# A GRU kernel in which TensorE gets the new state as two summands, and a search whose sums are queued inside the next products

## The reference, cut to what matters

```python
# block 1: a weighted outer product, of which the 5120 largest of each batch's 512 x 512 values become 1, the rest 0
adj = fside * cond[:, None, :] * softmax(x, -1) / sqrt(512);  adj[diagonal] = -inf
x = x + top_k_mask(adj, 5120)
# block 2: attention with 16 heads, conditioned norm
x = x + attention_block(x, cond, ...)
# block 3: a GRU over the 512 rows of x, starting from cond
for t in range(512):
    gi = x[:, t] @ W_ih + b_ih;  gh = h @ W_hh + b_hh
    r = sigmoid(i_r + h_r);  z = sigmoid(i_z + h_z);  n = tanh(i_n + r * h_n)
    h = (1 - z) * n + z * h;  hs[:, t] = h
x = x + hs
# block 4: linear sampling of x along its columns at places given by cond
```

## Time and profile before

| | |
|---|---|
| three runs | 2466.45, 2470.41, 2475.15 us (median 2470.41) |
| profiled execution | 2475.3 us, of which the span of instructions 2473.6 |
| PE busy | 2243.5 us, 91% of the span, 58517 matmuls |
| DVE busy | 1854.6 us, 75% |
| ACT busy | 1295.0 us, 52% |
| POOL busy | 532.7 us, 22% |
| granted TensorE clock, mean | 0.991 |

### The profile page before, as it was taken

One profiled execution on the slowest core, in us unless ns is written; L12 is line 12 of the kernel. 1 busy time (PEld: TensorE's weight loads), 2 busy tenths in 40 slices (PEclk: granted clock), 3 DMA queues, 4 the chain that ended last, 5 costly groups with the idle time before them and its releaser, 6 DMA issues.

```text
span 2473.6 us, 139634 instructions
## 1 busy us (share of the span) xinstructions
PE 2243.5 (91%) x58517; PEld 1912.7 (77%) x58517; DVE 1854.6 (75%) x8525; ACT 1295.0 (52%) x5693; POOL 532.7 (22%) x2223
## 2 busy tenths in 40 slices
PE   2668899898987899999999999999999999999998
PEld 2564454555544598988999999999999999999996
DVE  7876877868679588877787777777777768777775
ACT  5564856848557444444445454444444445444443
POOL 1001011020113323333222222222222222222221
PEclk9999899999999999999999999999999999999999
DMA  5000000010010000000000000000000000000000
GB/s 189 3 2 1 1 1 1 2 52 1 1 52 1 18 5 5 5 5 5 5 5 5 9 9 5 9 9 5 9 5 9 9 5 9 9 5 9 5 13 20
DMA packets 8444, 32.08 MB, mean 13 GB/s; under 512 B 836, under 2 KB 904, under 8 KB 7560
## 3 DMA queue, kind: packets, MB, share of 16 engines
q1 hardware_dynamic: 7392, 23.07, 2.5%
q10 hardware_dynamic: 424, 0.07, 0.0%
HBM read 18.94 MB, written 4.19 MB: 9 GB/s over the span
## 4 chain that ended last, share of the span: by engine, by line
PE 48%; DVE 9%; issue 2%; ACT 1%; POOL 1%; DVEq 0%; POOLq 0%
PE psum L1790 41%; PE psum L1723 5%; PE psum L1750 2%; DVE keepB L1423 1%; ACT mixA L822 1%; DVE nlineA L1415 1%; DVE nlineB L1415 1%; DVE rzA L1400 1%; PE psum L1472 1%; DVE keepA L1423 1%; POOL region_rows L486 1%; DVE parts1A L1432 0%; DVE parts0A L1432 0%; DVE lineA L1439 0%; DVEq L1431 0%
## 5 line engine op out<-in xcount | busy, mean ns | idle before, releaser
L1790 PE MATMUL psum<-parts0A,region_w_hh 128*128 128x40 f16 x12288 | 432.5, 179 | 16.2 <-DVE parts0A L1448 10.1
L1790 PE MATMUL psum<-parts1A,region_w_hh 128*128 128x40 f16 x12288 | 433.2, 179 | 15.3 <-DVE parts1A L1448 10.8
L1790 PE MATMUL psum<-parts1B,region_w_hh 128*128 128x40 f16 x12288 | 433.2, 179 | 7.3 <-issue 1.7
L1790 PE MATMUL psum<-parts0B,region_w_hh 128*128 128x40 f16 x12288 | 432.7, 179 | 7.4 <-DVE parts0B L1448 2.5
L822 ACT ACTIVATE mixA<-rzA 128x8 f32<-128x8 f32 x512 | 110.8, 216 | 564.3 <-DVE rzA L1400 564.1
L1790 PEld LDWEIGHTS psum<-parts0A,region_w_hh 128*128 128x128 f16 x12288 | 372.7, 96 | 25.6 <-DVE parts0A L1448 15.8
L1790 PEld LDWEIGHTS psum<-parts1A,region_w_hh 128*128 128x128 f16 x12288 | 373.3, 96 | 24.7 <-DVE parts1A L1448 16.7
L1790 PEld LDWEIGHTS psum<-parts0B,region_w_hh 128*128 128x128 f16 x12288 | 362.7, 96 | 26.2 <-DVE parts0B L1448 6.4
L1790 PEld LDWEIGHTS psum<-parts1B,region_w_hh 128*128 128x128 f16 x12288 | 362.7, 96 | 25.6 <-DVE parts1B L1448 6.0
L1400 DVE TENSOR_REDUCE rzA<-psum 128x8 f32<-128x32 f32 x512 | 97.6, 191 | 185.9 <-PE psum L1790 176.3
L497 POOL TENSOR_TENSOR addA<-zA,lineA 128x8 f32<-128x8 f32 x512 | 104.4, 204 | 586.8 <-ACT zA L829 586.8
(11 more groups left out here) (259 smaller groups left out, 4006.2 us busy)
## 6 DMA issues: line engine op xcount, KB each, us to landing
region_rows<-in_x_dram SPq DMA_DIRECT2D x4, 1024.0 KB, 12.4
out_dram<-region_w_b SPq DMA_DIRECT2D x16, 256.0 KB, 2.0
region_w_a<-in_L_cond_W_qkv_dram SPq DMA_DIRECT2D x1, 3072.0 KB, 22.7
region_w_hh<-in_L_cond_W_hh_dram SPq DMA_DIRECT2D x4, 768.0 KB, 7.2
region_rows<-in_L_cond_W_ih_dram SPq DMA_DIRECT2D x1, 3072.0 KB, 10.1
region_cond<-in_cond_dram SPq DMA_DIRECT2D x2, 1024.0 KB, 6.4
region_cols<-in_L_cond_W_emb_dram SPq DMA_DIRECT2D x1, 2048.0 KB, 18.4
region_w_out<-in_L_cond_W_out_dram SPq DMA_DIRECT2D x1, 1024.0 KB, 21.5
```

The source lines that it names most:

```text
L1790: made = e.matmul(k.slots(bank)[:, :, ch, :, 0:2], k.w16[:, 2 * read + c, part, NC * "rzn".index(g) + 2 * half + ch], k.parts[now][read][: ...
```

## The change

PE now multiplies the state as a sum of two terms that were never added for it: z h, and keep times tanh. Each has a high and a low fp16 part, so a chunk has 16 columns instead of 8, and with `COPIES` = 2 a matmul has 32 columns instead of 40. A group in PSUM is six columns: four products, the constant, the input's share; sums and the n line run over 48 columns.

POOL makes z h in fp32 (`zh`), the same product in fp16 (`zhigh`), and their difference (`zlow`), straight into the parts that PE reads; its copies to the array of states are gone. DVE makes keep times tanh in fp16 (`dve_high`) and in fp32 (`dve_cand`), both plain products of 8 columns, their difference (`dve_low`), and the state as `cand + zh` (`dve_state`), off the way to PE: that of A behind keep B, that of B behind low B. High no longer waits for z h. PE waits for `low` and `zlow` of a half. The products run through PSUM, so the state is still the sum.

In the search, PE does the first 10 of the 16 pieces of count n, then the total of count n - 1, then the other 6. The totals lie in banks 4 to 7 now, and `pe_embed`, which uses bank 7, waits until the last sign is made.

```diff
--- before.py
+++ after.py
@@ -40,7 +40,8 @@
 FAR = 2.0 ** 24
-COPIES = 5
+COPIES = 2
+COLUMNS = 6
 
...
@@ -295,14 +296,16 @@
         self.bias_in = small("bias_in", 2, GATES, 2)
-        self.parts = [[small(f"parts{parity}{half}", 2, B, 2, dtype=FP16) for half in "AB"] for parity in range(2)]
+        self.parts = [[small(f"parts{parity}{half}", 2, B, 4, dtype=FP16) for half in "AB"] for parity in range(2)]
         self.rz = [small(f"rz{h}", 2, 2, B) for h in "AB"]
         self.z = [small(f"z{h}", 2, B) for h in "AB"]
-        self.mix = [small(f"mix{h}", 2, B, 4) for h in "AB"]
-        self.nline = [small(f"nline{h}", 2, B, 4) for h in "AB"]
-        self.keep = [small(f"keep{h}", 2, B, 2) for h in "AB"]
-        self.add = [small(f"add{h}", 2, B, 2) for h in "AB"]
-        self.line = [small(f"line{h}", 2, B, 2) for h in "AB"]
+        self.mix = [self.head_power[:, 2 * i:2 * i + 2].rearrange("p t n -> p (t n)")[:, 0:12 * B].rearrange(
+            "p (c b q) -> p c b q", c=2, b=B) for i in range(2)]
+        self.nline = [t[:, 0:12 * B].rearrange("p (c b q) -> p c b q", c=2, b=B) for t in (self.top, self.neg_top)]
+        self.keep = [small(f"keep{h}", 2, B) for h in "AB"]
+        self.tanh = [small(f"tanh{h}", 2, B) for h in "AB"]
+        self.cand = [small(f"cand{h}", 2, B) for h in "AB"]
+        self.zh = [small(f"zh{h}", 2, B) for h in "AB"]
         self.rows_out = view("w_b", 0, FP32, 4, D)
...
@@ -475,8 +477,6 @@
         pool_zh(e, k, st, 1)
-        pool_state(e, k, st, 0)
-        pool_state(e, k, st, 1)
         if st < 96:
@@ -491,17 +491,15 @@
 def pool_zh(e, k, st, half):
...
     h = "AB"[half]
+    old, parts = k.state[:, st, 2 * half:2 * half + 2], k.parts[(st + 1) % 2][half]
     e.wait_ge(s[f"zsig{h}"], st + 1)
     if st:
-        e.wait_ge(s[f"line{h}"], st)
-    e.tensor_tensor(k.add[half][:, :, :, 1], k.z[half][:], k.line[half][:, :, :, 1], ALU.mult).then_inc(s[f"zh{h}"], 1)
-
-
-def pool_state(e, k, st, half):
-    s = k.sem
-    h = "AB"[half]
-    e.wait_ge(s[f"line{h}"], st + 1)
-    e.tensor_copy(k.state[:, st + 1, 2 * half:2 * half + 2], k.line[half][:, :, :, 1]).then_inc(s[f"state{h}"], 1)
+        e.wait_ge(s[f"state{h}"], st)
+    e.tensor_tensor(k.zh[half][:], k.z[half][:], old, ALU.mult).then_inc(s[f"zh{h}"], 1)
+    e.tensor_tensor(parts[:, :, :, 3], k.z[half][:], old, ALU.mult).then_inc(s[f"zhigh{h}"], 1)
+    e.wait_ge(s[f"zhigh{h}"], st + 1)
+    e.wait_ge(s[f"zh{h}"], st + 1)
+    e.tensor_tensor(parts[:, :, :, 2], k.zh[half][:], parts[:, :, :, 3], ALU.subtract).then_inc(s[f"zlow{h}"], 1)
 
 def act_program(e, k):
...
@@ -833,7 +831,7 @@
     e.wait_ge(s[f"nline{h}"], st + 1)
-    e.activation(k.add[half][:, :, :, 0], k.nline[half][:, :, :, 3], ACT.Tanh, scale=unscale).then_inc(s[f"tanh{h}"], 1)
+    e.activation(k.tanh[half][:], k.nline[half][:, :, :, 5], ACT.Tanh, scale=unscale).then_inc(s[f"tanh{h}"], 1)
 
 def dve_program(e, k):
...
@@ -1374,14 +1372,16 @@
         dve_high(e, k, st, 0, nxt)
-        dve_line(e, k, st, 0)
+        dve_cand(e, k, st, 0)
         dve_z_sum(e, k, st, 1)
...
         dve_keep(e, k, st, 1)
+        dve_state(e, k, st, 0)
         dve_high(e, k, st, 1, nxt)
-        dve_line(e, k, st, 1)
+        dve_cand(e, k, st, 1)
         dve_low(e, k, st, 1, nxt)
+        dve_state(e, k, st, 1)
         if 26 <= ss < 26 + NC and q + 2 < CHUNKS:
@@ -1412,15 +1412,15 @@
     e.wait_ge(s[("n_productsA", "rsigB")[half]], st + 1)
-    e.tensor_tensor_scan(k.nline[half][:].rearrange("p c b q -> p (c b q)"), k.mix[half][:].rearrange("p c b q -> p (c b q)"),
-                         k.bank(N_BANK[half], 8 * B), 0.0, ALU.mult, ALU.add).then_inc(s[f"nline{h}"], 1)
+    e.tensor_tensor_scan(k.nline[half].rearrange("p c b q -> p (c b q)"), k.mix[half].rearrange("p c b q -> p (c b q)"),
+                         k.bank(N_BANK[half], 2 * B * COLUMNS), 0.0, ALU.mult, ALU.add).then_inc(s[f"nline{h}"], 1)
 
...
 def dve_keep(e, k, st, half):
...
     e.wait_ge(s[f"zsig{h}"], st + 1)
-    e.tensor_scalar(k.keep[half][:, :, :, 1], k.z[half][:], 1.0, k.minus_h_scale[:], ALU.subtract, ALU.mult).then_inc(s[f"keep{h}"], 1)
+    e.tensor_scalar(k.keep[half][:], k.z[half][:], 1.0, k.minus_h_scale[:], ALU.subtract, ALU.mult).then_inc(s[f"keep{h}"], 1)
 
 def dve_high(e, k, st, half, nxt):
@@ -1428,25 +1428,30 @@
     e.wait_ge(s[f"keep{h}"], st + 1)
+    e.tensor_tensor(k.parts[nxt][half][:, :, :, 1], k.tanh[half][:], k.keep[half][:], ALU.mult).then_inc(s[f"high{h}"], 1)
+
+
+def dve_cand(e, k, st, half):
+    s = k.sem
+    h = "AB"[half]
+    e.tensor_tensor(k.cand[half][:], k.tanh[half][:], k.keep[half][:], ALU.mult).then_inc(s[f"cand{h}"], 1)
+
+
+def dve_low(e, k, st, half, nxt):
+    s = k.sem
+    h = "AB"[half]
+    e.wait_ge(s[f"cand{h}"], st + 1)
+    e.wait_ge(s[f"high{h}"], st + 1)
+    e.tensor_tensor(k.parts[nxt][half][:, :, :, 0], k.cand[half][:], k.parts[nxt][half][:, :, :, 1],
+                    ALU.subtract).then_inc(s[f"low{h}"], 1)
+
+
+def dve_state(e, k, st, half):
+    s = k.sem
+    h = "AB"[half]
     e.wait_ge(s[f"zh{h}"], st + 1)
-    e.tensor_tensor_scan(k.parts[nxt][half][:].rearrange("p c b q -> p (c b q)"), k.keep[half][:].rearrange("p c b q -> p (c b q)"),
-                         k.add[half][:].rearrange("p c b q -> p (c b q)"), 0.0, ALU.mult, ALU.add).then_inc(s[f"high{h}"], 1)
-
-
-def dve_line(e, k, st, half):
-    s = k.sem
-    h = "AB"[half]
-    e.tensor_tensor_scan(k.line[half][:].rearrange("p c b q -> p (c b q)"), k.keep[half][:].rearrange("p c b q -> p (c b q)"),
-                         k.add[half][:].rearrange("p c b q -> p (c b q)"), 0.0, ALU.mult, ALU.add).then_inc(s[f"line{h}"], 1)
-
-
-def dve_low(e, k, st, half, nxt):
-    s = k.sem
-    h = "AB"[half]
-    e.wait_ge(s[f"line{h}"], st + 1)
-    e.wait_ge(s[f"high{h}"], st + 1)
-    e.tensor_tensor(k.parts[nxt][half][:, :, :, 0], k.line[half][:, :, :, 1], k.parts[nxt][half][:, :, :, 1],
-                    ALU.subtract).then_inc(s[f"low{h}"], 1)
+    e.wait_ge(s[f"cand{h}"], st + 1)
+    e.tensor_tensor(k.state[:, st + 1, 2 * half:2 * half + 2], k.cand[half][:], k.zh[half][:], ALU.add).then_inc(s[f"state{h}"], 1)
 
 def pe_program(e, k):
@@ -1454,8 +1459,7 @@
     e.transpose(k.bank(7, VEC_ROWS), k.vec_rows, k.ident[0:VEC_ROWS, 0:VEC_ROWS]).then_inc(s["vec"], 1)
-    for n in range(COUNTS):
-        pe_count(e, k, n)
+    pe_search(e, k)
 
@@ -1475,6 +1479,7 @@
 def pe_embed(e, k):
     s = k.sem
+    e.wait_ge(s["signed"], COUNTS - FIRST_HIGH)
     e.wait_ge(s["w_emb_in"], 16)
@@ -1484,15 +1489,40 @@
 
-def pe_count(e, k, n):
+PAIRS_AHEAD = 10
+
+
+def pe_count(e, k, n, cs):
     s = k.sem
     b = n % B
-    e.wait_ge(s["mask_made"], n + 1)
-    for c in range(PER // P):
+    if cs[0] == 0:
+        e.wait_ge(s["mask_made"], n + 1)
+        if n >= B:
+            e.wait_ge(s["sum_copied"], n - B + 1)
+    for c in cs:
         made = e.matmul(k.bank(b, 2), k.masks[b][:, c], k.ones16[:, 0:2], start=(c == 0), stop=(c == PER // P - 1))
-    made.then_inc(s["mask_summed"], 1)
+    if cs[-1] == PER // P - 1:
+        made.then_inc(s["mask_summed"], 1)
+
+
+def pe_sum(e, k, n):
+    s = k.sem
+    b = n % B
     e.wait_ge(s["sum_copied"], n + 1)
-    e.matmul(k.bank(b, 4)[:, 2:3], k.ones16[:], k.counts[:, b:b + 1], start=True, stop=True).then_inc(s["counted"], 1)
+    if n == FIRST_HIGH - 1:
+        e.wait_ge(s["vec"], 2)
+    e.matmul(k.bank(4 + b, 4)[:, 2:3], k.ones16[:], k.counts[:, b:b + 1], start=True, stop=True).then_inc(s["counted"], 1)
+
+
+def pe_search(e, k):
+    for n in range(COUNTS):
+        pe_count(e, k, n, range(PAIRS_AHEAD))
+        if n and n != FIRST_HIGH:
+            pe_sum(e, k, n - 1)
+        pe_count(e, k, n, range(PAIRS_AHEAD, PER // P))
+        if n == FIRST_HIGH - 1:
+            pe_sum(e, k, n)
+    pe_sum(e, k, COUNTS - 1)
 
 def pe_places(e, k, b):
@@ -1775,6 +1805,7 @@
                     e.wait_ge(s[f"low{u[0]}"], st)
+                    e.wait_ge(s[f"zlow{u[0]}"], st)
             first = (h, g) not in started
@@ -1787,8 +1818,8 @@
                     for part in range(2):
-                        made = e.matmul(k.slots(bank)[:, :, ch, :, 0:2], k.w16[:, 2 * read + c, part, NC * "rzn".index(g) + 2 * half + ch],
-                                        k.parts[now][read][:, c].unsqueeze(1).broadcast_to([P, COPIES, B, 2]),
+                        made = e.matmul(k.slots(bank)[:, :, ch, :, 0:4], k.w16[:, 2 * read + c, part, NC * "rzn".index(g) + 2 * half + ch],
+                                        k.parts[now][read][:, c].unsqueeze(1).broadcast_to([P, COPIES, B, 4]),
                                         start=first and ch == c == part == 0, stop=(read == 1), skip_group_check=True)
```

More of the change, by code:

```diff
@@ L57 @@
 r_productsA z_productsA n_productsA r_productsB z_productsB n_productsB
-rsumA zsumA nlineA rsigA zsigA tanhA keepA zhA highA lineA lowA stateA putA
-rsumB zsumB nlineB rsigB zsigB tanhB keepB zhB highB lineB lowB stateB putB
```

(26 more changed lines are left out.)

7 lines of the change are left out of this document (3 added, 4 removed).

## The result

The changed kernel takes 2515.63 us (median of 4 runs, 2512.0 to 2524.78), the kernel before 2469.94 beside it: a ratio of 1.0189, 95% interval 1.0155 to 1.0222. It is 46 us slower, where 12 us faster was forecast. The profiled span is 2510.3 us, 36.7 over the one before: the profiled execution is the slowest of the four before and the fastest of the four after, so that the two profiles show 9 us less than the medians.

What follows compares the result with a forecast made beforehand. Bound: the recurrence's closed chain of waits (3.00 us a step), then the search's mask spacing. Search -25, embedding +0.5, chain +10, DVE jobs +4, sampling -2 gave -12.5 us: 2458 us, own range 2445 to 2470, eight in ten 2436 to 2500.

Steps and rivals of the forecast that it cites:

- PE's second wait: Recurrence, PE waiting for POOL's low part: met 0.15 us before the other, hidden; at most 25 us in all.
- The prediction's own sign: Recurrence: median distance of two r sums of A, 3.03 us if right, 3.08 or more for rival 1.
- rival 1: Recurrence: POOL and DVE collide, two operations stretched 0.04 us each a step, +41 us, total 2499; chance 0.18.
- The sampling steps and DVE's jobs: Recurrence: -2 us in 16 steps with POOL's big additions, +4 us where 44 long DVE jobs are pushed 0.09 each.
- The end of +8: Sampling steps: upper end of the -2 us term, if the state addition stands behind POOL's addition of 1.26 us.
- the 44 longest jobs: First 96 steps: DVE jobs of 0.68 to 0.75 us at step's end, pushed 0.09 each by the state addition, +4 us.
- The rule against the change: Recurrence: by the shared port pair, DVE's new two-SBUF-input products and additions would stand behind POOL's six products a step.
- the search: Search for the 5120th value: mask period falls from 0.88 to 0.67 us, saving 25 us; embedding wait adds 0.5.
- the chain of the undisturbed step: Recurrence: longer sums and scan, shorter products on the chain of waits, +0.02 us a step, +10 us.
- PE's half B starts behind DVE's low and not POOL's: Recurrence: sign that PE's wait on half B is ended by DVE's low part, not by POOL.
- The clock: Recurrence: sign that PE's clock stays at 1.00 from 861 us on; its fall was a rival, +144 us, chance 0.04.

Runs made afterwards that it cites:

- e2: The changed kernel with POOL's and DVE's low parts counting up one semaphore, so PE waits once a half, not twice: 2474.45 us, ratio 0.9996.
- e3: The kernel before with a second, redundant PE wait at each half, for DVE's line, met 0.2 us before low ends: 2525.74 us, ratio 1.0197.
- e11: The kernel before with one more PE wait at each half's head, for the previous step's r sigmoid, met over 1 us early: 2518.92 us, ratio 1.0166.
- e4: The changed kernel with three copies instead of two, so 48 columns a matmul: 2520.81 us, ratio 1.0181.
- e8: The kernel before with 4 copies in place of 5, so 32 columns a matmul, not 40: 2474.14 us, ratio 1.0007.
- e6: The kernel before with the new search, and PE's waits for r sum, z sum and n line removed: 2443.28 us, ratio 0.9870.
- e7: The changed kernel with one wait for both low parts, B's state addition moved behind the next z sum A, same six PE waits removed: 2461.42 us, ratio 0.9946.

## Why the prediction was wrong

**The step that failed** is the one on PE's second wait: "hidden; a wait in the queue costs nothing when it is met early, and at most the 0.05 us of one wait instruction, 25 us in all". That it is met early was right (0.12 us, 0.15 said). That it then costs nothing was wrong: its 1022 instructions cost 37 us of the recurrence (after against e2), 47 in e3, 49 in e11 (48, 49 and 41 by the ratios), that is 0.036 to 0.048 us each. Taking out 511 others gave less, 5 and 7 us by the ratios, 0.01 us each. Even the bound was short, because it counted one such wait a step where there are two, and it was left out of the range. The cost isn't on the chain of an undisturbed step, where I looked, but in PE's gaps at one place in 256 of its instructions, where no row of the chain shows it. The earlier trace rows have no row of PE's wait instructions; the view of waits had the hint, 16.1 us of idle weight loads that end with "issue".

The prediction's own sign misled here: a median distance of r sums of 3.08 or more was to mean rival 1, POOL and DVE in each other's way. It came at 3.115, and the kernel was slower, as rival 1 had it, but e2 has the same operations on POOL and DVE and 3.028. The sign could not tell the two causes apart.

**The sampling steps and DVE's jobs**, -2 and +4, cost 12.6 us together (e2 against before: 319.2 for 305.0 us in the first 96 steps, less 1.6 for the chain). The end of +8 "if the state addition stands behind the addition of 1.26 us" is what happened: the 31 steps with an addition or behind one took 110.3 us for 103.8. The other 65 took 7.7 more, 1.1 of it by the chain. The rest of that lies in steps with a job on DVE; that the state addition pushes more than the 44 longest jobs is the likely reason, not tested by itself.

The rule against the change I had as rival 1, outside the sum. The Trainium skill (SBUF — State Buffer, section "SBUF: two separate sides") has GpSimd and a VectorE operation with two SBUF inputs lock each other out for a whole instruction. The stretched addition agrees with it. Beside POOL's small products it showed nothing: high is at 0.18, cand at 0.16. So rival 1 did not come, with its +0.08 a step on small operations.

**Right were** the search (0.66 for 0.67 us a mask, 24.1 of 24.5 us net), the chain of the undisturbed step (the medians of its parts add up to 3.024 us, to 3.007 before: +0.017 where +0.02 was taken; r sum 0.208, n line 0.254, products 0.16 to 0.18), and that PE's half B starts behind DVE's low and not POOL's. The clock did not stay at 1.00, but e3, e4 and e8 show that this is not where the time is. The sum as it came, of the two profiled executions: search -24.1, chain +9, first 96 steps +12.6, wait instructions +37, behind the recurrence +1.5, together +36 of the 36.7. The 9 us by which the medians are further apart are in no term.

## What to carry to other kernels

Where an engine issues small instructions back to back, count its wait instructions before adding a semaphore: let two producers count up one semaphore, drop waits that another one implies (a small gain here, by e6 and e7), or place a wait where a weight load without one can carry it. Read the "issue" rows of the waits, not only the chain of one clean step. And keep small two-input VectorE operations of the critical path out from under long GpSimd ones.
